# A strip loop's value unit issued straight behind the scores, and a unit's decays ahead of ScalarE's first copy

## The chip, the cores and the metric

The kernel runs on one core of a Trainium2 chip. The metric is the device time of the program, in microseconds (us). Five engines work side by side, each through its own instructions in order, and wait for each other on semaphores: TensorE (PE: matmuls, its weight loads in rows PEld), VectorE (DVE), ScalarE (ACT), GpSimd (POOL) and SyncE (SP, which issues DMAs). The kernel before took 2348.93 us, the median of 3 runs (2347.29 to 2349.18).

## The reference, cut to what matters

One layer over 32 batches of 64 tokens of width 256: cross-attention to 1601 context rows for each batch, a selective scan, and 64 experts with top-8 routing. The change lies in the attention:

```
q  = qdq(layernorm(x)) @ qdq(wq).T + bq          # 16 heads of 16
k, v = split(ctx @ wkv.T + bkv)                  # 1601 rows of 256 each
attn = softmax(q @ k.T / 4)
o    = attn @ v
x    = x + qdq(o) @ qdq(wp).T + bp
x    = x + scan(layernorm(x)) ; x = x + experts(layernorm(x))
# scan: h = exp(dt * A) * h + dt * x * B ; y = h . C
```

## The kernel before, in words

The tokens go in 16 pairs of batches (128 tokens). The attention of a pair is 16 strips: for each batch, each half of the heads (step), 4 strips of two heads each. A strip is 128 rows (two heads by 64 tokens) against 1604 key columns. One loop over G runs through the strips, one slot for each G; what the text calls slot s is G modulo 16. In a slot:

- TensorE: `scores(G)` (12 matmuls into the four-bank tensor S, line 618); `turn(G, 0..3)`: the probabilities of strip G-1 turned by 13 transposes in four groups of 4 or 3 (line 628); `v_mm`: a unit of values, two tiles of 128 context rows (line 601), in slots 1 to 7 for the pair's second batch and 9 to 15 for the next pair's first; `times_v(G)`: 12 to 16 products of turned probabilities and values into O (line 646); `k_mm(G + 4)`: the keys of a strip four ahead (line 591). Slots 0 and 8 have no value unit (`NO_VALUES`).
- ScalarE: `ot_up_` copies a finished O, `turned(G, k)` copies the four turned groups to SBUF (line 780), `soft(G)` takes the exponential of S (line 788), `k_up` writes the rounded keys (line 772), `decay` writes exp(dt A) of one scan unit (line 805, 4 instructions in each of slots 8 to 15).
- VectorE: `strip_max(G)` (line 958, 1604 columns of S), `v_up` copies a value unit to SBUF (line 952), `k_low` writes the keys' remainder (line 942), and between these the mixer work of the pair before: norms, routing (`rest_a`, `rest_b`) and the scan units (`scan_unit`).

S must be read by both `strip_max` and `soft` before the next scores may overwrite it. Everything else that TensorE writes, other than O, goes through a ring of three PSUM banks W0 to W2 (`BANKS = 3`). `jobs_at(G)` lists a slot's jobs in TensorE's order: T (a turned group), V (a value unit), K (keys) and small ones (O, oqT, proj, ln2T, xp, dt, XQ, Q, yT, ln3T, logits, pos, from the table `MIX` by slot and place). Job n takes bank n modulo 3, and `take` makes TensorE wait until job n-3 has been copied out: by ScalarE if that was a T, by VectorE otherwise (`freed_by`). So the order of jobs decides which copy each job waits for. In `jobs_at`, place 0 lies between the second and the third turned group, place 1 behind the fourth, place 2 behind the keys. Nothing plans at run time: the order is written out. Each engine's order has to agree with the list.

Of the kernel before, what the change touches and what calls it, by code (L numbers as in the profile page):

```python
# [60 lines left out]
UNITS = 2 * NS // QS  # L61
FIRST_DECAY = 4
# [16 lines left out]
def in_flight(G):  # L79

    return [(G - 1 - k, k) for k in range(STRIPS) if 0 <= G - 1 - k < ALL_STRIPS]


def values_at(G):

    i, slot = divmod(G, SLOTS)
    if 1 <= slot <= 7 and i < PAIRS:
        return i, 1, slot - 1
    if slot >= 9 and i + 1 < PAIRS:
        return i + 1, 0, slot - 9  # L90
    return None
# [20 lines left out]
def jobs_at(G):  # L112

    turns = [("T", G, k) for k in range(STRIPS)] if 0 < G <= ALL_STRIPS else []
    v = [("V",) + values_at(G)] if values_at(G) else []
    keys = [("K", G + STRIPS)] if G + STRIPS < ALL_STRIPS else []
    if G % SLOTS in NO_VALUES:
        return turns + small_at(G, 0) + keys + small_at(G, 1)
    return turns[:2] + small_at(G, 0) + v + turns[2:] + small_at(G, 1) + keys + small_at(G, 2)


def freed_by(job):
# [83 lines left out]
def mixer_phase(nc, io, dram):  # L206
    with ExitStack() as ctx:
# [338 lines left out]
        def _(pe):  # L546
# [181 lines left out]
            for G in range(END):  # L728
                if G < ALL_STRIPS:
                    scores(G)  # L730
                if 0 < G <= ALL_STRIPS:
                    turn(G, 0)
                    turn(G, 1)
                if G % SLOTS in NO_VALUES:
                    if 0 < G <= ALL_STRIPS:
                        turn(G, 2)
                        turn(G, 3)
                    if in_flight(G):
                        times_v(G)
                    small(G, 0)  # L740
                else:
                    small(G, 0)
                    if values_at(G):
                        v_mm(*values_at(G))
                    if 0 < G <= ALL_STRIPS:
                        turn(G, 2)
                        turn(G, 3)
                    small(G, 1)
                    if in_flight(G):
                        times_v(G)  # L750
                if G + STRIPS < ALL_STRIPS:
                    k_mm(G + STRIPS)
                small(G, 1 if G % SLOTS in NO_VALUES else 2)
# [3 lines left out]
        def _(act):  # L757
# [54 lines left out]
            for G in range(END):  # L812
                p, m = mixer_at(G)
                strip = 0 < G <= ALL_STRIPS
                if 0 <= G - STRIPS - 1 < ALL_STRIPS:
                    ot_up_(G - STRIPS - 1)
                if strip:
                    turned(G, 0)
                    turned(G, 1)
                if strip and G % SLOTS in NO_VALUES:  # L820
                    turned(G, 2)
                scanned = p is not None and 0 <= m - FIRST_DECAY < UNITS
                if scanned:
                    decay(p, m - FIRST_DECAY, 0)
                if G < ALL_STRIPS:
                    soft(G)
                if m == 3 and p is not None:
# [10 lines left out]
                    turned(G, 3)  # L838
                if G + STRIPS < ALL_STRIPS:
                    k_up(G + STRIPS)  # L840
                if scanned:
                    decay(p, m - FIRST_DECAY, 1)
                if m == 14 and p is not None:

                    act.wait_ge(dve_up, dve_at(p, "LOGITS"))
# [6 lines left out]
        def _(dve):  # L852
# [282 lines left out]
            for G in range(END):  # L1135
                i, slot = divmod(G, SLOTS)
                p, m = mixer_at(G)
                mix, nxt = p is not None, i + 1 < PAIRS
                v = values_at(G)
                if G < ALL_STRIPS:  # L1140
                    strip_max(G)
                if m == 0:
                    link = Chain(dve, dve_b, p, B_LINKS, pause[:]) if mix else None
                for job in small_at(G, 0):
                    if job[0] == "O":
                        norm_o(job[1])
                if slot == 8 and nxt:
                    x_up(i + 1)
                if mix and m < 15:
                    rest_a(p, m, link)  # L1150
                if v:
                    v_up(*v)
                if slot == 8 and i >= 2:
                    route_end(i - 2, route_link)
                if mix and m == 15:
# [423 lines left out]
```

## Time and profile before

| | |
|---|---|
| median of 3 runs | 2348.93 us |
| the profiled execution | 2351.5 us |
| its span (first to last instruction) | 2349.8 us |
| PE busy | 2113.0 us (90%) |
| DVE busy | 1754.1 us (75%) |
| ACT busy | 1439.1 us (61%) |
| mean granted TensorE clock | 0.968 of 2.4 GHz |
| exponentials, line 788 | 256, 1599 ns each |
| row maxima, line 958 | 256, 1820 ns each |
| value copies, line 952 | 224, 650 ns each |

The strip loop fills most of the span, the experts and the combination follow from about 1880 us on. The busy share of TensorE counts overlapping, pipelined matmuls; where it stands near the whole of a stretch, the engine has hardly any gap there. A timeline row gives the start of a group of like instructions, the time from its first start to its last end, the engine, the line and the operation, and in brackets the idle time of the engine just before with what ended it. On TensorE the next group starts before the last one's end, so intervals are best taken from start to start.

### The profile page before, as it was taken

How to read it: one execution, taken by the hardware profiler on the slowest of the kernel's cores; microseconds unless marked ns; L12 is line 12 of the kernel's file. 1: busy time of each engine (PE TensorE's matmuls, PEld its weight loads, DVE VectorE, ACT ScalarE, POOL GpSimd, SP SyncE). 2: the span in 40 equal slices, each digit the busy share in tenths (PEclk: the TensorE clock that was granted, in tenths of full speed). 3: DMA queues.
4: the chain of work that ended last, by engine and by line, in shares of the span. 5: the costliest groups of instructions: out<-in, count | busy, mean ns of one | idle time of the engine just before them, and what ended most of it. 6: DMA issues, size and time to landing. Idle time of an engine off the chain costs nothing. (4 is left out here: it accounts for less than half of the span.)

```text
span 2349.8 us, 56067 instructions
## 1 busy us (share of the span) xinstructions
PE 2113.0 (90%) x21448; PEld 1465.6 (62%) x21448; DVE 1754.1 (75%) x3728; ACT 1439.1 (61%) x3012; POOL 679.3 (29%) x710
## 2 busy tenths in 40 slices
PE   5999999999999999999999999999994099989966
PEld 3666666666666666666666666666663077767644
DVE  4557888879797978888887979797887555555536
ACT  1667776768676767677776768676775044434423
POOL 1002040303031221303040303131221447767760
PEclk9999999999999999999999999999997599999988
DMA  6465763323231313232232323131311165566638
GB/s 190 192 241 208 273 209 127 103 57 115 76 87 70 91 70 86 79 100 89 74 102 54 106 81 93 70 89 68 89 52 46 48 189 184 185 208 190 190 104 322
DMA packets 132712, 294.17 MB, mean 125 GB/s; under 512 B 21899, under 2 KB 89143, under 8 KB 126304
## 3 DMA queue, kind: packets, MB, share of 16 engines
q1 hardware_dynamic: 114016, 255.89, 34.8%
q0 software_dynamic: 18432, 34.69, 4.2%
q8 instruction: 174, 2.85, 0.5%
q14 instruction: 90, 0.74, 0.1%
HBM read 165.40 MB, written 108.27 MB: 116 GB/s over the span
## 5 line engine op out<-in xcount | busy, mean ns | idle before, releaser
L788 ACT ACTIVATE sb_probs<-S,sb_negmax 128x1604 f32<-128x1604 f32 x256 | 409.3, 1599 | 225.0 <-DVE sb_negmax L958 224.5
L780 ACT ACTIVATE sb_probsT<-W 128x384 f32<-128x384 f32 (+1 forms) x1024 | 473.5, 513 | 68.0 <-PE W L628 65.3
L628 PE MATMUL W<-sb_ident,sb_probs 128*128 128x128 f32 (+1 forms) x3328 | 478.6, 280 | 29.1 <-DVE sb_ln2T L980 15.5
L958 DVE TENSOR_REDUCE sb_negmax<-S 128x1 f32<-128x1604 f32 x256 | 465.9, 1820 | 1.3
L628 PEld LDWEIGHTS W<-sb_ident,sb_probs 128*128 128x128 f32 (+1 forms) x3328 | 363.7, 139 | 147.8 <-issue 68.5
L601 PE MATMUL W<-sb_wkv_in,sb_ctx 128*128 128x256 f32 (+1 forms) x1664 | 409.4, 388 | 4.8 <-ACT sb_probsT L780 2.6
L591 PE MATMUL W<-sb_ctx,sb_wkv_in 128*32 128x401 f32 x4096 | 398.0, 503 | 3.0 <-DVE sb_V L952 3.0
L601 PEld LDWEIGHTS W<-sb_wkv_in,sb_ctx 128*128 128x128 f32 (+1 forms) x1664 | 292.9, 186 | 67.2 <-ACT sb_probsT L780 19.1
L772 ACT ACTIVATE sb_K_hi<-W,sb_pair_cols 128x401 fp32r<-128x401 f32 x256 | 152.9, 597 | 238.8 <-PE W L591 238.8
L1292 POOL DMA_INDIRECT y_scratch<-sb_ys,sb_places x256 | 261.4, 1021 | 113.3 <-issue 62.9
L942 DVE SCALAR_TENSOR_TENSOR sb_K_lo<-W,sb_pair_cols,sb_K_hi 128x401 fp32r<-128x401 f32 x256 | 161.9, 632 | 153.6 <-ACT sb_K_hi L772 153.3
L500 POOL TENSOR_TENSOR sb_bx<-sb_u,sb_BC 128x512 f32<-128x512 f32 x128 | 164.8, 1304 | 363.8 <-DVE sb_u L1081 233.1
L646 PE MATMUL O<-sb_probsT,sb_V 128*32 128x128 f32 (+1 forms) x6656 | 243.9, 276 | 0.0
L591 PEld LDWEIGHTS W<-sb_ctx,sb_wkv_in 128*32 128x32 f32 x4096 | 131.5, 110 | 115.1 <-issue 102.9
L646 PEld LDWEIGHTS O<-sb_probsT,sb_V 128*32 128x32 f32 (+1 forms) x6656 | 173.2, 109 | 47.8 <-issue 34.8
L952 DVE COPY sb_V<-W 128x512 f32<-128x512 f32 (+1 forms) x224 | 145.7, 650 | 42.2 <-PE W L601 38.9
L512 POOL DMA_INDIRECT xe_scratch<-sb_row,sb_sc_idx x128 | 139.9, 1093 | 43.8 <-issue 31.0
L1364 ACT ACTIVATE sb_ys<-Y 128x512 f32<-128x512 f32 x64 | 38.3, 598 | 180.1 <-DMA y_scratch<-sb_ys,sb_places 170.3
L618 PEld LDWEIGHTS S<-sb_K_hi,sb_Q_hi 32*128 32x128 f32 x1024 | 49.6, 181 | 158.1 <-issue 155.6
L1332 PE MATMUL Y<-sb_wd,sb_hid 96*128 96x256 f32 x512 | 126.6, 391 | 16.5 <-DVE sb_ys L1406 16.4
L528 POOL TENSOR_TENSOR sb_st<-sb_st,sb_neg_half 128x1 f32<-128x1 f32 x16 | 8.8, 548 | 416.7 <-DVE sb_st L1062 416.7
L523 POOL TENSOR_TENSOR sb_st<-sb_st,sb_neg_half 128x1 f32<-128x1 f32 x16 | 9.1, 567 | 397.1 <-DVE sb_st L874 397.1
(187 smaller groups left out, 2951.4 us busy)
## 6 DMA issues: line engine op xcount, KB each, us to landing
sb_ctx<-ctxT SPq DMA_DIRECT2D x32, 1604.0 KB, 7.7
xe_scratch<-sb_none SPq DMA_DIRECT2D x32, 1088.0 KB, 12.6
sb_xg<-xe_scratch SPq DMA_DIRECT2D x64, 544.0 KB, 4.2
sb_BC<-bc_scratch SPq DMA_DIRECT2D x32, 1024.0 KB, 6.3
sb_Q_hi<-sb_q_hi SPq DMA_DIRECT2D x128, 128.0 KB, 4.2
sb_Q_lo<-sb_q_lo SPq DMA_DIRECT2D x128, 128.0 KB, 5.1
y_scratch<-sb_none SPq DMA_DIRECT2D x16, 1024.0 KB, 11.3
sb_rows<-y_scratch SPq DMA_DIRECT2D x16, 1024.0 KB, 8.5
```

What stands on the lines that cost most here:

```text
L500: pool.tensor_tensor(bx[:, mine, :], u[:, h, :].unsqueeze(1).to_broadcast([P, QS, P]), BC[:, mine, :], ALU.mult).then_inc(pool_up, 1)
L591: ins = pe.matmul(W[32 * c:32 * c + 32, 0:CK], wkv_in[:, k, w0:w0 + 32], ctx_t[b][:, k, c * CK:(c + 1) * CK], start=(k == 0), stop=(k == D ...
L601: ins = pe.matmul(W[0:keys_in(t), n * D:(n + 1) * D], ctx_t[b][:, k, t * P:t * P + keys_in(t)], wkv_in[:, k, D:2 * D], start=(k == 0), sto ...
L628: ins = pe.transpose(W[0:keys_in(t), at * P:(at + 1) * P], probs[n % 2][:, t * P:t * P + keys_in(t)], ident[:])
L646: ins = pe.matmul(O[32 * s:32 * s + 32, 0:P], V[b][0:keys_in(t), t, g * P + 32 * s:g * P + 32 * s + 32], probsT[k][n % (k + 1)][0:keys_in( ...
L772: act.activation(K_hi[:, s, 0:CK], ring[bank_of("K", n)][:, 0:CK], ACT.Identity, bias=pair_cols[:, g * STRIPS + s:g * STRIPS + s + 1]).the ...
L780: act.activation(probsT[k][n % (k + 1)][:, 0:wide], ring[bank_of("T", G, k)][:, 0:wide], ACT.Copy)\
L788: act.activation(probs[n % 2][:].rearrange("p (c k) -> p c k", c=QUADS), scores_of, ACT.Exp, bias=negmax[:, slot:slot + 1], accum_out=den[ ...
L942: dve.scalar_tensor_tensor(K_lo[:, s, 0:CK], bank("K", n)[:, 0:CK], pair_cols[:, g * STRIPS + s:g * STRIPS + s + 1], K_hi[:, s, 0:CK].bitc ...
L952: dve.tensor_copy(V[b][0:keys_in(tiles[-1]), tiles[0]:tiles[-1] + 1, :].rearrange("p t d -> p (t d)"), bank("V", pair, b, unit)[0:keys_in( ...
L958: dve.tensor_reduce(negmax[:, slot:slot + 1], scores_of, AX.XY, ALU.max, negate=True).then_inc(max_done, 1)
L1292: pool.indirect_dma_start(dram["y"], bass.IndirectOffsetOnAxis(ap=places[e % 4][:, c:c + 1], axis=0), ys[n][:, c, :], None, bounds_check=T ...
```

## The change

In every slot with a value unit, the unit's matmuls are issued right behind the scores, ahead of all four turned groups, where before they stood between the second and the third. VectorE copies the unit right behind the row maximum, ahead of the small copies and the mixer's work at that place. The list `jobs_at` is changed accordingly, and with it which job precedes which by three in the ring. Apart from this, ScalarE does all four decay instructions of a unit in one piece behind `ot_up_`, ahead of the first copy of turned probabilities; before, two stood ahead of the exponential and two behind `k_up`.

```diff
@@ jobs_at
-    return turns[:2] + small_at(G, 0) + v + turns[2:] + small_at(G, 1) + keys + small_at(G, 2)
+    return v + turns[:2] + small_at(G, 0) + turns[2:] + small_at(G, 1) + keys + small_at(G, 2)
@@ tensor
                 if G < ALL_STRIPS:
                     scores(G)
+                if values_at(G):
+                    v_mm(*values_at(G))
                 if 0 < G <= ALL_STRIPS:
                     turn(G, 0)
                     turn(G, 1)
...
                     small(G, 0)
-                    if values_at(G):
-                        v_mm(*values_at(G))
                     if 0 < G <= ALL_STRIPS:
                         turn(G, 2)
                         turn(G, 3)
@@ scalar
                     ot_up_(G - STRIPS - 1)
+                if p is not None and 0 <= m - FIRST_DECAY < UNITS:
+                    for part in range(2):
+                        decay(p, m - FIRST_DECAY, part)
                 if strip:
                     turned(G, 0)
                     turned(G, 1)
                 if strip and G % SLOTS in NO_VALUES:
                     turned(G, 2)
-                scanned = p is not None and 0 <= m - FIRST_DECAY < UNITS
-                if scanned:
-                    decay(p, m - FIRST_DECAY, 0)
...
                 if G + STRIPS < ALL_STRIPS:
                     k_up(G + STRIPS)
-                if scanned:
-                    decay(p, m - FIRST_DECAY, 1)
@@ vector
                     link = Chain(dve, dve_b, p, B_LINKS, pause[:]) if mix else None
+                if v:
+                    v_up(*v)
                 for job in small_at(G, 0):
...
                     rest_a(p, m, link)
-                if v:
-                    v_up(*v)
```

How instructions stand on TensorE in slot 15 of a pair, before. S are the scores, `W<-sb_ident,sb_probs` the turned groups, `W<-sb_wkv_in,sb_ctx` the value unit, `W<-sb_ctx,sb_wkv_in` the keys; `ring_free_act` and `ring_free_dve` say whose copy the bank is waited for:

```order
L618 MATMUL S<-sb_K_hi,sb_Q_lo 128x400 x3
L628 MATMUL W<-sb_ident,sb_probs 128x128 [waits exp_done,ring_free_act]
L628 MATMUL W<-sb_ident,sb_probs 128x128 x2
L628 MATMUL W<-sb_ident,sb_probs 128x128 [waits ring_free_act]
L628 MATMUL W<-sb_ident,sb_probs 128x128 x3
L601 MATMUL W<-sb_wkv_in,sb_ctx 128x256 [waits ctx_in0,ring_free_dve]
L601 MATMUL W<-sb_wkv_in,sb_ctx 128x256 x3
L628 MATMUL W<-sb_ident,sb_probs 128x128 [waits ring_free_act]
L628 MATMUL W<-sb_ident,sb_probs 128x128 x2
L628 MATMUL W<-sb_ident,sb_probs 128x128 [waits ring_free_act]
```

The same place now:

```order
L618 MATMUL S<-sb_K_hi,sb_Q_lo 128x400 x3
L601 MATMUL W<-sb_wkv_in,sb_ctx 128x256 [waits ctx_in0,ring_free_act]
L601 MATMUL W<-sb_wkv_in,sb_ctx 128x256 x3
L628 MATMUL W<-sb_ident,sb_probs 128x128 [waits exp_done,ring_free_act]
L628 MATMUL W<-sb_ident,sb_probs 128x128 x2
L628 MATMUL W<-sb_ident,sb_probs 128x128 [waits ring_free_dve]
L628 MATMUL W<-sb_ident,sb_probs 128x128 x3
L628 MATMUL W<-sb_ident,sb_probs 128x128 [waits ring_free_dve]
L628 MATMUL W<-sb_ident,sb_probs 128x128 x2
L628 MATMUL W<-sb_ident,sb_probs 128x128 [waits ring_free_act]
```

The value unit is ahead; the third turned group now takes the value unit's own bank and waits for VectorE's copy of it, where before it waited for ScalarE's copy of the first group, and the keys took the value unit's bank.

ScalarE in slot 15, before, from the exponential of one strip to the next (`sb_soft<-sb_dt_,sb_A` are the decays, `sb_OT<-O` is `ot_up_`):

```order
L772 ACTIVATE sb_K_hi<-W,sb_pair_cols 128x401 [waits s_done,ring_full]
L805 ACTIVATE sb_soft<-sb_dt_,sb_A 128x128 x2
L797 ACTIVATE sb_OT<-O 32x128 [waits pv_done]
L780 ACTIVATE sb_probsT<-W 128x384 [waits pv_done,ring_full]
L780 ACTIVATE sb_probsT<-W 128x512 [waits pv_done,ring_full]
L805 ACTIVATE sb_soft<-sb_dt_,sb_A 128x128 [waits dve_up]
L805 ACTIVATE sb_soft<-sb_dt_,sb_A 128x128
L788 ACTIVATE sb_probs,sb_den<-S,sb_negmax 128x1604 [waits ring_full,max_done]
```

And now:

```order
L772 ACTIVATE sb_K_hi<-W,sb_pair_cols 128x401 [waits s_done,ring_full]
L797 ACTIVATE sb_OT<-O 32x128 [waits pv_done]
L805 ACTIVATE sb_soft<-sb_dt_,sb_A 128x128 [waits dve_up]
L805 ACTIVATE sb_soft<-sb_dt_,sb_A 128x128 x3
L780 ACTIVATE sb_probsT<-W 128x384 [waits pv_done,ring_full]
L780 ACTIVATE sb_probsT<-W 128x512 [waits pv_done,ring_full]
L788 ACTIVATE sb_probs,sb_den<-S,sb_negmax 128x1604 [waits ring_full,max_done]
```

The decays of a unit stand in one piece ahead of the first two copies, and nothing stands between those and the exponential.

VectorE in slot 7, before (`sb_z<-W` reads the small job dt, `sb_u` is the end of the chain that the decays need):

```order
L958 TENSOR_REDUCE sb_negmax<-S 128x1 [waits s_done]
L1020 TENSOR_SCALAR sb_z<-W,sb_cols 128x128 [waits ring_full]
L1021 TENSOR_SCALAR sb_z<-W,sb_cols 128x128 [waits dve_b]
L1024 SCALAR_TENSOR_TENSOR sb_soft<-sb_z 128x256 [waits ring_free_dve]
L952 COPY sb_V<-W 128x512 [waits pv_done,ring_full]
L1075 TENSOR_SCALAR sb_soft<-sb_soft 128x256 [waits act_up]
```

And now (the same functions, two lines earlier in the file):

```order
L956 TENSOR_REDUCE sb_negmax<-S 128x1 [waits s_done]
L950 COPY sb_V<-W 128x512 [waits pv_done,ring_full]
L1018 TENSOR_SCALAR sb_z<-W,sb_cols 128x128 [waits ring_full]
L1019 TENSOR_SCALAR sb_z<-W,sb_cols 128x128 [waits dve_b]
L1022 SCALAR_TENSOR_TENSOR sb_soft<-sb_z 128x256 [waits ring_free_dve]
L1073 TENSOR_SCALAR sb_soft<-sb_soft 128x256 [waits act_up]
```

The copy of the value unit stands ahead of the three instructions that read dt.

## Rows read from the trace of the kernel before

**Rows 1.** The page, busy time of each engine (share of the span), instructions.
```profile
PE 2113.0 (90%) x21448; PEld 1465.6 (62%) x21448; DVE 1754.1 (75%) x3728; ACT 1439.1 (61%) x3012; POOL 679.3 (29%) x710
```

**Rows 2.** Windows: one pair; stretch, its length, busy us, granted clock, DMA share, GB/s.
```profile
1025.23:1134.92 109.69, 106.10 (x1228) 71.98 (x1224) 92.53 (x195) 78.03 (x164) 24.82 (x23) 1.00 0.29 85
```

**Rows 3.** Timeline, TensorE: first scores of pair 1 and of pair 15.
```profile
150.85 0.46 PE L618 MATMUL S<-sb_K_hi,sb_Q_hi 32*128 32x402 f32 x4
...
1683.36 0.45 PE L618 MATMUL S<-sb_K_hi,sb_Q_hi 32*128 32x402 f32 x4
```

**Rows 4.** Waits of TensorE in that pair: us in total, times, longest.
```profile
PE W L628 <- DVE sb_ln2T L980: 1.1, 1, 1.1
```

**Rows 5.** Timeline, TensorE, a slot 15 and the start of the next slot.
```profile
1019.00 0.46 PE L618 MATMUL S<-sb_K_hi,sb_Q_hi 32*128 32x402 f32 x4
...
1019.76 0.98 PE L628 MATMUL W<-sb_ident,sb_probs 128*128 128x128 f32 x7
1020.58 1.92 PE L601 MATMUL W<-sb_wkv_in,sb_ctx 128*128 128x256 f32 x8
1022.33 0.82 PE L628 MATMUL W<-sb_ident,sb_probs 128*128 128x128 f32 x6
...
1025.23 0.45 PE L618 MATMUL S<-sb_K_hi,sb_Q_hi 32*128 32x402 f32 x4
```

**Rows 6.** Timeline, VectorE, the same slot 15.
```profile
1019.82 0.63 DVE L942 SCALAR_TENSOR_TENSOR sb_K_lo<-W,sb_pair_cols,sb_K_hi 128x401 fp32r<-128x401 f32 x1
1020.36 1.82 DVE L958 TENSOR_REDUCE sb_negmax<-S 128x1 f32<-128x1604 f32 x1
1022.53 0.69 DVE L952 COPY sb_V<-W 128x512 f32<-128x512 f32 x1 [0.35 <-PE W L601]
```

**Rows 7.** Timeline, ScalarE, the same slot 15.
```profile
1020.63 0.98 ACT L780 ACTIVATE sb_probsT<-W 128x384 f32<-128x384 f32 x2
1021.50 0.69 ACT L805 ACTIVATE sb_soft<-sb_dt_,sb_A 128x128 f32<-128x128 f32 x2
1022.22 1.60 ACT L788 ACTIVATE sb_probs<-S,sb_negmax 128x1604 f32<-128x1604 f32 x1
```

**Rows 8.** Timeline, TensorE, slot 1 (from 1030.50) and slot 3 (from 1045.69).
```profile
1030.50 0.46 PE L618 MATMUL S<-sb_K_hi,sb_Q_hi 32*128 32x402 f32 x4
...
1034.36 0.93 PE L628 MATMUL W<-sb_ident,sb_probs 128*128 128x128 f32 x7
...
1045.69 0.45 PE L618 MATMUL S<-sb_K_hi,sb_Q_hi 32*128 32x402 f32 x4
...
1048.98 0.82 PE L628 MATMUL W<-sb_ident,sb_probs 128*128 128x128 f32 x6
...
1050.78 1.55 PE L591 MATMUL W<-sb_ctx,sb_wkv_in 128*32 128x401 f32 x16 [0.18 <-DVE sb_V L952]
```

**Rows 9.** Timeline, VectorE, slots 1 and 3.
```profile
1032.22 1.82 DVE L958 TENSOR_REDUCE sb_negmax<-S 128x1 f32<-128x1604 f32 x1
...
1048.29 1.83 DVE L958 TENSOR_REDUCE sb_negmax<-S 128x1 f32<-128x1604 f32 x1
1050.04 0.68 DVE L952 COPY sb_V<-W 128x512 f32<-128x512 f32 x1
```

**Rows 10.** Timeline, TensorE, slot 10, the small job O.
```profile
987.97 0.33 PE L656 MATMUL W<-sb_ident,sb_OT 128*128 128x128 f32 x1 [0.80 <-DVE sb_K_lo L942]
```

**Rows 11.** Timeline, ScalarE, slot 8 (its scores start at 972.53).
```profile
973.98 1.36 ACT L780 ACTIVATE sb_probsT<-W 128x512 f32<-128x512 f32 x3 [0.41 <-PE W L628]
975.21 0.70 ACT L805 ACTIVATE sb_abar<-sb_dt_,sb_A 128x128 f32<-128x128 f32 x2
```

**Rows 12.** Timeline, TensorE, 13 transposes at clock 1.0, and at 0.5.
```profile
1776.96 1.96 PE L628 MATMUL W<-sb_ident,sb_probs 128*128 128x128 f32 x13
...
1781.77 3.06 PE L628 MATMUL W<-sb_ident,sb_probs 128*128 128x128 f32 x13 [2.06 <-ACT sb_probs L788]
```

**Rows 13.** Windows: the experts and the combination, columns as in rows 2.
```profile
1900.00:2350.00 450.00, 386.71 (x1852) 292.04 (x1849) 248.16 (x571) 178.48 (x370) 275.88 (x321) 0.94 0.61 198
```

## The prediction, made before the changed kernel ran

> **What bounds the kernel now.** First the page's busy times: TensorE has 90% of the span, VectorE 75%, ScalarE 61% [rows 1]. Then the windows, pair by pair: of a pair's 109.69 us TensorE is busy for 106.10 at a granted clock of 1.00, VectorE for 92.53 [rows 2]. Its gaps make 3.6 us of the pair; the longest are 1.1 us in slot 6 [rows 4] and 0.8 us in slot 10, for VectorE's keys [rows 10]. So in the strip loop TensorE is the bound and has nearly no gap. The loop is regular: pair 1 starts at 150.85 and pair 15 at 1683.36, 14 pairs in 1532.5 us [rows 3], 109.5 each. Last the timelines of single slots, from start to start on TensorE. Below, all times inside a slot count from the start of its scores.
>
> In slot 15 [rows 5] TensorE issues scores at 0, two turned groups at 0.76, the value unit at 1.58, the other two groups at 3.33, and the next scores at 6.23. VectorE [rows 6] starts the row maximum at 1.36. It does not wait for the scores there: it comes from the keys' remainder of the slot before (0.82 to 1.45), which comes from ScalarE's key copy, which comes from the end of TensorE's keys. The maximum takes 1.82, then VectorE stands 0.35 for the value unit and copies it from 3.53 to 4.22. Nobody waits for that copy but the keys, which come behind the products.
>
> **The change, part by part.** The work is the same: no matmul, copy or DMA is added or removed, and no DMA queue is touched. Only the order moves, and with it the banks.
>
> *The value unit first.* Issuing V ahead of two groups costs TensorE nothing by itself; the sum of the three is the same, 3.33 us to the third group in slot 15. What changes is who waits for the copy. With three banks and V, T0, T1, T2 in line, T2 gets V's bank. It waits for VectorE's copy, which stands behind the row maximum. Where a small job stands behind T1, that job gets V's bank and waits instead, with T2 behind it in line. The earliest issue of that job after the scores is
>
> start of the maximum + 1.75 (the next VectorE instruction starts that long after it: 1048.29 to 1050.04, rows 9) + 0.68 (the copy) + 0.06 (the copy's end at 1050.72 to the keys that waited for it at 1050.78, rows 8 and 9) = start of the maximum + 2.49.
>
> In slot 15 that is 1.36 + 2.49 = 3.85 against 3.33 [rows 5, 6]: 0.5 us of stall. Behind the waiting T2 stand T3, the products, the keys and the next scores; the keys' end then sets the next key copy, remainder and maximum. Nothing in this chain can catch up: it is the loop's new cycle, 1.36 + 2.49 + 2.9 (third group to next scores) = 6.75 us. The 0.35 us that VectorE stood for V goes, but it stands ahead of a later wait now, for the keys.
>
> The same reading in each of the 14 slots with a value unit (of each the start of the maximum and of the third group; the first and the last, slots 1 and 15, have their rows, and slot 3). Where VectorE's backlog of scan work delays its maximum today (slots 10 to 12, 14 and 0, up to 0.9 us), the longer slots clear it, and I take the maximum at 1.34 to 1.43 there.
>
> - Slots 9, 11, 12, 13, 15: +0.64, +0.23, +0.28, +0.49, +0.50 = +2.14.
> - Slots 10 and 14, with the small job O: slot 10 today waits for the keys' remainder until 987.97 [rows 10]; that wait goes with the backlog: -0.24. Slot 14 has a short unit, +0.07. Together -0.17.
> - Slot 1: maximum at 1.72 [rows 9], small job at 4.24, third group at 4.51 against 3.86 [rows 8]: +0.65. In the same way slots 2, 4, 5, 6, 7: +0.50, +0.27, +0.42, +0.69, +0.59. Together +3.12. In slot 6 the fourth group already waits for VectorE today, so only the difference counts.
> - Slot 3: VectorE starts the maximum at 2.60, since it normalises the next queries ahead of it [rows 9]. Third group at 5.09 against 3.29 [rows 8]: 1.80; today the keys wait for the same copy [rows 8], which takes back 0.35: +1.44.
>
> *The decays ahead of the first copy.* In slots 9 to 15 this is hidden. ScalarE has done the key copy and `ot_up_` at about 1.05, four decays take 1.3 (0.69 for two, rows 7), so it is free at 2.35. T0 now comes behind V, so its copy can start at about 3.1, as against 1.63 [rows 7]. The exponential moves: today it starts at 3.22 [rows 7], now behind T1's copy at about 3.95. It ends at about 5.65, and the next scores come at 6.7 or later, so a full 1 us of cover is left. T3's copy ends at about 6.5, the next key copy wants ScalarE at 6.9: 0.4 us of cover, the thinnest. If it is gone, each 0.1 us late there is 0.1 us on every slot.
>
> In slot 8 there is no V to hide it. T3 needs the bank of T0, and T0's copy starts at 1.45 today [rows 11]. Now four decays stand ahead of it, and they wait for the end of the softplus chain of slot 7, which on VectorE moves back too (dt waits for the value copy, 1.41 + 2.49 = 3.9 as against 1.6). The chain also waits for ScalarE's exponential, which ends about as late as dt's readers, so I get the chain's end at 1.0, decays to 2.3, T0's copy to 2.9, T3 at 2.95 against 2.1: +0.85. Bounds: not below 0.85, since `ot_up_` ends at 1.05 anyway; up to 2.3 if the chain moves by as much as dt does beyond the slot's own growth (2.3 - 0.6 = 1.7), which would be 23 us in all.
>
> In slot 0 two decays of slot 15 no longer stand ahead of the first copies: -0.26.
>
> **Sum.** 2.14 - 0.17 + 3.12 + 1.44 + 0.85 - 0.26 = 7.12 us for each pair. For the 14 pairs from 1 to 14: 100. Pair 0 has no mixer work but the same norms of queries, and slots 2, 3 and 6 where these delay the maximum; the same reading gives 8. Pair 15 has no value units from slot 9 on: 6. Together 114 us. The profiled execution took 2351.5 us (its span 2349.8), so 2465.5 there, a factor 1.0485; on the median of 2348.93 that is 2463 us. The copies, groups and handoffs are measured; the starts of the maximum are what can be wrong. 0.1 us on them is 14 x 16 x 0.1 = 22 us in all. From both sides: if the maximum starts as today everywhere with no backlog cleared, some 1.5 us per pair more, +24; if the wait is shorter by 0.15 in each slot, -33.
>
> **The rivals.**
>
> *TensorE's clock falls* (8%). Today the loop runs at 1.00, which is 2.4 GHz, with waits of at most about 1 us. The same 13 transposes took 1.96 us at that clock and 3.06 behind a wait of 2.06 us, in a stretch granted 0.5, which is 1.2 GHz [rows 12]. In the stretch of experts, with TensorE busy 86% of the time, the mean is 0.94, so 12% of it is at the lower level [rows 13]. After the change the loop would be busy for 106.1 of 116.8 us, 91%, in gaps of half a microsecond to 1.8. If 12% of 1740 us fell to the lower level, each at 1.56 times the duration, 75 us come on top: 2538 us. Against it: waits of 0.8 and 1.1 us occur in each pair today [rows 4, 10] and the clock stays at 1.00 [rows 2].
> The Trainium skill, "TensorE: Matmul & The Clock Gate", section "A second HAM failure mode: psum-queue depth-cycling", describes this: a kernel that cycles through PSUM banks and idles briefly between its groups of matmuls was seen to swing between the clock's two levels. By that rule 2538 would be the forecast; the trace's loop, which cycles through three banks and idles briefly, does not agree so far, at 1.00 throughout.
>
> *ScalarE becomes late as well* (10%). The cover of 0.4 us ahead of the next key copy is gone, say by 0.3 us, in the 13 ordinary slots. That delays the maximum and with it the copy: 13 x 0.3 x 16 = 62 us on top, 2525.
>
> *VectorE gets ahead, and it is faster* (5%). If the value copy no longer waits for V, VectorE saves 0.35 in each scan slot; if that let the maximum start right at the scores' end, at 0.87 or earlier, the copy would be done when T2 wants its bank (0.87 + 2.49 = 3.36), and the wait in slot 10 and a few others would go, about 1 us a pair, 15 us: 2334. The point that decides is the start of the maximum: below 0.87 it is faster, above it a stall. Against it: the maximum stands behind the keys' remainder, which ends at 1.45 at the earliest and does not come sooner by this change.
>
> *It does nothing* (5%): the turned groups find their banks free because the copy comes earlier than I read, 2349.
>
> **How the numbers follow.** The forecast has 72%, the others 8, 10, 5 and 5. Within 0.2% is about what a measurement of this kernel can tell from no change. Slower by more than that: 72 + 8 + 10 = 90%; within: 5%; faster: 5%. Range: 2465 less 33 and some room for slots 3 and 8 gives 2425; upwards 24 and most of the way to the late ScalarE, 2515, which also takes in slot 8's upper bound. That holds the forecast and half of that rival.
>
> **What would show it.** In the profile after: TensorE's waits get a large new entry, transposes (line 628, and the small jobs) for VectorE's value copy (line 950), some 200 times and 100 to 150 us in total; a slot 15 of about 6.75 us; slot 3 of about 8.3; a pair of about 116.8; VectorE's wait for the value unit gone; the exponential starting at about 3.95 behind the copy of T1, not behind the maximum. ScalarE's wait for the keys stays above zero in ordinary slots. The clock at 1.00 in the loop. The prediction is wrong if the maximum starts well before 1.3, or if the third group is not held by the copy, or if ScalarE has no idle time left before line 772.

## The result and the profile after

The changed kernel took 2466.2 us (median of 4 runs, 2460.53 to 2472.05) against 2349.05 (4 runs, 2347.29 to 2349.94): a ratio of 1.0501, 95% interval 1.0486 to 1.0516. It is 117 us slower; the prediction said 2463 and 114. The profiled execution has a span of 2470.3 us. In experiment 1 below, one of four runs took 2932 us at a mean granted clock of 0.674; the other three took 2455.87 to 2459.42 us at 0.967 to 0.969, and its ratio is from these.

One pair in the windows view of the changed kernel (columns as in rows 2):

```profile
1095.45:1212.09 116.64, 105.36 (x1224) 72.36 (x1220) 92.42 (x195) 78.16 (x164) 24.08 (x23) 1.00 0.27 79
```

Against [rows 2] TensorE's and VectorE's work is the same and the pair is 6.95 us longer. The waits of TensorE in that pair:

```profile
PE W L628 <- DVE sb_V L950: 3.4, 6, 1.6
PE W L656 <- DVE sb_V L950: 3.3, 4, 1.1
PE W L663 <- DVE sb_V L950: 3.2, 3, 2.0
PE W L628 <- ACT sb_probsT L780: 0.8, 1, 0.8
PE W L691 <- DVE sb_V L950: 0.4, 1, 0.4
```

Fourteen waits, one for each slot with a value unit, are for VectorE's value copy: 10.3 us in a pair where [rows 2] has 3.6 us of gaps of all kinds. Over the whole loop there are 214 such waits, 155 us in all; the prediction said some 200 and 100 to 150 us. In a pair they are more than the 6.95 us of growth, since they take the place of most of those gaps. The one wait for ScalarE is slot 8's.

The timeline of TensorE in a slot 15 (answers to [rows 5]):

```profile
1088.60 0.46 PE L618 MATMUL S<-sb_K_hi,sb_Q_hi 32*128 32x402 f32 x4
...
1089.35 2.00 PE L601 MATMUL W<-sb_wkv_in,sb_ctx 128*128 128x256 f32 x8
1091.18 0.93 PE L628 MATMUL W<-sb_ident,sb_probs 128*128 128x128 f32 x7
1092.50 0.87 PE L628 MATMUL W<-sb_ident,sb_probs 128*128 128x128 f32 x6 [0.39 <-DVE sb_V L950]
...
1095.45 0.46 PE L618 MATMUL S<-sb_K_hi,sb_Q_hi 32*128 32x402 f32 x4
```

and VectorE there (answers to [rows 6]):

```profile
1090.03 1.82 DVE L956 TENSOR_REDUCE sb_negmax<-S 128x1 f32<-128x1604 f32 x1
1091.76 0.68 DVE L950 COPY sb_V<-W 128x512 f32<-128x512 f32 x1
```

The copy ends at 1092.44, the third group starts at 1092.50. The 0.35 us for which VectorE stood before the value unit are gone. The slot takes 6.85 us, as against 6.23. ScalarE there (answers to [rows 7]):

```profile
1089.65 1.28 ACT L805 ACTIVATE sb_soft<-sb_dt_,sb_A 128x128 f32<-128x128 f32 x4
1091.71 1.03 ACT L780 ACTIVATE sb_probsT<-W 128x384 f32<-128x384 f32 x2 [0.78 <-PE W L628]
1092.64 1.59 ACT L788 ACTIVATE sb_probs<-S,sb_negmax 128x1604 f32<-128x1604 f32 x1
...
1095.59 0.60 ACT L772 ACTIVATE sb_K_hi<-W,sb_pair_cols 128x401 fp32r<-128x401 f32 x1 [0.51 <-PE W L591]
```

The decays are hidden here (0.78 us idle behind them), the exponential starts at 4.04 us of the slot, and 0.51 us of cover are left ahead of the keys. Slot 3, where the maximum is late, has the row that answers to [rows 8]:

```profile
1121.75 0.88 PE L628 MATMUL W<-sb_ident,sb_probs 128*128 128x128 f32 x6 [1.58 <-DVE sb_V L950]
```

The slots one by one, from start to start of the scores, medians over pairs 2 to 14 (before; growth as the prediction had it; growth as measured):

| slot | 0 | 1 | 2 | 3 | 4 | 5 | 6 | 7 |
|---|---|---|---|---|---|---|---|---|
| before, us | 5.27 | 6.89 | 8.30 | 6.84 | 7.04 | 7.91 | 8.03 | 6.72 |
| predicted | -0.26 | +0.65 | +0.50 | +1.44 | +0.27 | +0.42 | +0.69 | +0.59 |
| measured | -0.26 | +0.58 | +0.44 | +1.36 | +0.26 | +0.13 | +0.69 | +0.60 |

| slot | 8 | 9 | 10 | 11 | 12 | 13 | 14 | 15 |
|---|---|---|---|---|---|---|---|---|
| before, us | 6.52 | 6.48 | 7.36 | 6.49 | 6.67 | 6.34 | 6.61 | 6.22 |
| predicted | +0.85 | +0.64 | -0.24 | +0.23 | +0.28 | +0.49 | +0.07 | +0.50 |
| measured | +1.08 | +0.24 | -0.13 | +0.37 | +0.30 | +0.53 | +0.08 | +0.63 |

Sum: 7.12 predicted, 6.90 measured. Pair 0 grew by 8.8, pair 1 by 9.1 and pair 15, to its slot 14, by 3.2 us. Five stretches at the lower clock, told below, cost some 1.6 us each; one lies in pair 1 and is in its 9.1, the other four make the rest. The loop grew by 117.5 us.

### The profile page after: what moved, and what is told of

Its sections match the earlier page's. It is cut to its first block and busy times, and to the rows that moved or that the text cites. A ratio compares the mean times of both kernels' runs of the same rounds, so it can differ in the third digit from the quotient of the medians.

```text
span 2470.3 us, 56068 instructions
## 1 busy us (share of the span) xinstructions
PE 2110.6 (85%) x21448; PEld 1475.2 (60%) x21448; DVE 1751.3 (71%) x3728; ACT 1439.8 (58%) x3012; POOL 678.3 (27%) x710
## 5 line engine op out<-in xcount | busy, mean ns | idle before, releaser
L780 ACT ACTIVATE sb_probsT<-W 128x384 f32<-128x384 f32 (+1 forms) x1024 | 479.1, 519 | 337.5 <-PE W L628 336.6
L628 PE MATMUL W<-sb_ident,sb_probs 128*128 128x128 f32 (+1 forms) x3328 | 463.9, 276 | 75.7 <-DVE sb_V L950 54.4
L628 PEld LDWEIGHTS W<-sb_ident,sb_probs 128*128 128x128 f32 (+1 forms) x3328 | 370.6, 139 | 148.8 <-DVE sb_V L950 78.0
L601 PE MATMUL W<-sb_wkv_in,sb_ctx 128*128 128x256 f32 (+1 forms) x1664 | 416.9, 392 | 0.0
L646 PE MATMUL O<-sb_probsT,sb_V 128*32 128x128 f32 (+1 forms) x6656 | 249.8, 279 | 0.0
```

The source lines that it names most:

```text
L601: ins = pe.matmul(W[0:keys_in(t), n * D:(n + 1) * D], ctx_t[b][:, k, t * P:t * P + keys_in(t)], wkv_in[:, k, D:2 * D], start=(k == 0), sto ...
L628: ins = pe.transpose(W[0:keys_in(t), at * P:(at + 1) * P], probs[n % 2][:, t * P:t * P + keys_in(t)], ident[:])
L646: ins = pe.matmul(O[32 * s:32 * s + 32, 0:P], V[b][0:keys_in(t), t, g * P + 32 * s:g * P + 32 * s + 32], probsT[k][n % (k + 1)][0:keys_in( ...
L780: act.activation(probsT[k][n % (k + 1)][:, 0:wide], ring[bank_of("T", G, k)][:, 0:wide], ACT.Copy)\
```

## The experiments

Each is compared with the kernel before on the same chip (2348 us there).

**1. The value unit first, the decays in their old place.**

```diff
@@ the changed kernel, scalar
-                if p is not None and 0 <= m - FIRST_DECAY < UNITS:
-                    for part in range(2):
-                        decay(p, m - FIRST_DECAY, part)
...
+                scanned = p is not None and 0 <= m - FIRST_DECAY < UNITS
+                if scanned:
+                    decay(p, m - FIRST_DECAY, 0)
                 if G < ALL_STRIPS:
                     soft(G)
...
                     k_up(G + STRIPS)
+                if scanned:
+                    decay(p, m - FIRST_DECAY, 1)
```

> The value unit first, as in the changed kernel, but the decays where they were before. Theory (the stall is the third ring job's wait for VectorE's value copy): the placement alone costs nearly all of the 117 us, 2465 us (2450 to 2480). Slot 8 goes back to about 6.5 us, which gives back some 13 us, but in slots 9 to 15 two decays stand ahead of the exponential behind T1's late copy, so ScalarE is late for the next keys by 0.1 to 0.2 us, which takes it away again. Rival (the decays ahead of the first copy are what costs): back to within 20 us of the kernel before, below 2370 us.

Measured: 2459.08 us, ratio 1.0451 (1.0374 to 1.0528). The placement of the value unit alone costs some 110 of the 117 us. The rival falls. Slot 8 went back to 6.71 us, but slot 9 took 7.41 instead of the changed kernel's 6.72, so the two together gained 0.2 us, no more. About 3 of the 7 us between this run and the changed kernel are the clock: three stretches at the lower level here, five there. The total came out as forecast, but not by the way forecast: ScalarE did lose its idle time ahead of the keys in slots 11, 12, 13 and 15, yet these slots took 6.92, 6.97, 6.87 and 6.85 us, at most 0.06 more than in the changed kernel. What took slot 8's gain away was slot 9's late maximum (1.88 us into the slot, as against 1.18), see 5.

**2. The decays' part alone,** in the kernel before.

```diff
@@ the kernel before, scalar
                     ot_up_(G - STRIPS - 1)
+                if p is not None and 0 <= m - FIRST_DECAY < UNITS:
+                    for part in range(2):
+                        decay(p, m - FIRST_DECAY, part)
...
-                    decay(p, m - FIRST_DECAY, 0)
...
-                    decay(p, m - FIRST_DECAY, 1)
```

> The decays' part of the change alone: all four ahead of the first copy in slots 8 to 15, the value unit in its old place. Theory: slot 8 pays 0.85 to 1.1 us as in the changed kernel, slot 9 gives 0.2 back, slot 0 gives 0.26 back: some 10 us, 2359 us (2352 to 2366). Rival (the two parts need each other, and the decays cost little without the value unit first): within 5 us of 2349.

Measured: 2363.97 us, ratio 1.0067 (1.0050 to 1.0084), 16 us. The direction holds and the time is within the range, 5 us above its middle. Slot 8 grew by 0.93 and slot 9 shrank by 0.29, as expected; slots 10 and 14 grew by 0.37 and 0.21, which I had not seen; slot 11 shrank by 0.15; and slot 0 kept its 5.27 us.

**3. As 2, with slot 8 in its old order.**

```diff
-                if p is not None and 0 <= m - FIRST_DECAY < UNITS:
+                scanned = p is not None and 0 <= m - FIRST_DECAY < UNITS
+                if scanned and G % SLOTS not in NO_VALUES:
                     for part in range(2):
                         decay(p, m - FIRST_DECAY, part)
...
+                if scanned and G % SLOTS in NO_VALUES:
+                    decay(p, m - FIRST_DECAY, 0)
...
+                if scanned and G % SLOTS in NO_VALUES:
+                    decay(p, m - FIRST_DECAY, 1)
```

> The value unit in its old place behind T1; all four decays ahead of ScalarE's first copy in slots 9 to 15, old order in slot 8. Theory: T0 and T1 are copied late (2.35 instead of 1.63 us) but before T2 and T3 want their banks (3.33 and 3.8), and slot 0 loses the two decays in front of its first copies (5.27 to 5.01 us): 15 x 0.26 = 4 us less, 2345 us. Rival (moving decays ahead of copies always delays the copies' waiters): 10 us or more slower.

Measured: 2355.87 us, ratio 1.0025 (1.0004 to 1.0047). A miss: 8 us slower, not 4 faster. TensorE's waits in a pair show why:

```profile
PE W L628 <- DVE sb_ln2T L983: 1.1, 1, 1.1
PE W L601 <- ACT sb_probsT L780: 0.9, 1, 0.9
PE W L656 <- DVE sb_K_lo L945: 0.8, 1, 0.8
PE S L618 <- ACT sb_probs L788: 0.3, 1, 0.3
```

The second is new in this size (0.2 us in the kernel before): in slot 14 the value unit waits for ScalarE's copy of a turned group. With a small job behind T1, the old order gives the value unit T1's bank, and T1's copy now stands behind four decays. In the changed kernel the value unit is first and does not meet this. And slot 0 did not gain: with the decays out of ScalarE's way, the next scores wait for the exponential (the last of these rows), which stands behind a maximum that starts at 1.59. In the changed kernel VectorE's backlog is cleared and the maximum starts at 1.33. Run 1 has that earlier maximum with the decays in their old place, and its slot 0 takes 5.13 us. So the -0.26 in the changed kernel needs both parts: the decays alone give nothing, the maximum alone 0.14.

**4. As 3, with slots 10 and 14 in the old order too.**

```diff
-                if scanned and G % SLOTS not in NO_VALUES:
+                if scanned and G % SLOTS not in (8, 10, 14):
...
-                if scanned and G % SLOTS in NO_VALUES:
+                if scanned and G % SLOTS in (8, 10, 14):
```

> The value unit in its old place, the four decays ahead of ScalarE's first copy in slots 9, 11, 12, 13 and 15 only. In the run with slots 10 and 14 among them, these two grew by 0.37 and 0.20 us; reading: with a small job behind T1 the value unit takes T1's bank, and T1's copy had moved from 2.0 to 2.7 us. Theory: slots 10 and 14 go back to 7.36 and 6.61 us and the time to 2347 us (2343 to 2350). Rival (slot 10 grew because of slot 9's decays, not its own): slot 10 stays at 7.7 us, 2354.

Measured: 2351.58 us, ratio 1.0009 (1.0000 to 1.0018). Slots 10 and 14 took 7.36 and 6.61 us: the reading of T1's bank holds. The total came out above the range since slot 15 took 6.59 us, 0.37 more than before: it now has slot 14's last two decays and its own four ahead of its first copy. Slot 11 grew by 0.10 in the same place behind slot 10, and slot 12 gave that back. Slot 0 took 5.02 us here, with its maximum at 1.33 and no decays ahead of its copies, which bears out the reading in 3.

**5. The changed kernel with slot 8's decays in the old order** (the edit of 3, in the changed kernel).

> The changed kernel, with the decays of slot 8 (no value unit there) where they were before: two ahead of the exponential, two behind the keys. Theory: slot 8 of the changed kernel is 7.60 us against 6.52, because T0's copy stands behind four decays and T3 waits for T0's bank; slot 9 gained 0.4 us from it since VectorE had caught up. So about 0.8 us less a pair, 12 us: 2454 us, slot 8 at 6.5 to 6.7. Rival (slot 8 is long because VectorE's chain of slot 7 moved back): slot 8 stays above 7.2 us and the time within 5 us of 2466.

Measured: 2460.89 us, ratio 1.0464 (1.0404 to 1.0524). Slot 8 went to 6.71 us, so its 7.60 was T0's copy behind the decays. But slot 9 went from 6.72 to 7.41 and took 0.7 of the 0.9 us back. VectorE's long work in slot 8 (routing and the next queries) is followed by slot 9's maximum, which starts at 1.2 us of a slot 9 when slot 8 is long and at 1.9 when it is short. So the decays' net cost in the changed kernel is about 0.2 us a pair, 3 us in all. The forecast had counted all of slot 8's 0.8 us, and so the run came out 7 us above it. This run has four stretches at the lower clock instead of five.

**6. The value unit second,** between T0 and T1, ScalarE as in 5.

```diff
-    return v + turns[:2] + small_at(G, 0) + turns[2:] + ...
+    return turns[:1] + v + turns[1:2] + small_at(G, 0) + turns[2:] + ...
@@ tensor
+                if 0 < G <= ALL_STRIPS:
+                    turn(G, 0)
                 if values_at(G):
                     v_mm(*values_at(G))
                 if 0 < G <= ALL_STRIPS:
-                    turn(G, 0)
                     turn(G, 1)
```

> As the run before this one, with the value unit between the first and the second turned group: one ring job more now stands between it and the one that takes its bank (T3 or, with a small job ahead, T2). Theory: that job is due at about 3.8 us and the copy is done at 3.85, so ordinary slots lose about 0.1 us and only slots 2, 3, 6 and 9 much (0.3, 1.0, 0.4 and 0.2 us): 2375 us (2360 to 2390). Rival (any value unit ahead of its old place costs in proportion to how far it is moved): half of the loss stays, 2405 us.

Measured: 2404.21 us, ratio 1.0220 (1.0160 to 1.0280). The forecast of the total is missed, and by the total the rival is hit to the microsecond. The slots do not fit the rival, by which every slot would keep about half of its loss: slot 3 kept 1.03 of 1.36 us and slot 2 only 0.06 of 0.44, and slot 5 got shorter by 0.17. They fit the formula, but not my use of it. Slots 2, 3 and 6 grew by 0.06, 1.03 and 0.39 us. Slots 13 and 15 grew by 0.20 and 0.21 and not by 0.1: in slot 15 T3 starts at 3.66 us in the kernel before, so it is due well ahead of the 3.8 that I had estimated from the value unit's place; here it starts at 3.81, 0.05 us behind the copy's end, and the products behind it 0.21 us later than before. Slots 1 and 4, which I had left out, grew by 0.36 and 0.22: with a small job behind T1 it is T2 that takes the value unit's bank. In slot 1 the formula gives 1.72 + 2.49 = 4.21 for it, as against 3.86 before, and it starts at 4.19. Slots 8 and 9 grew by 0.39 and 0.60, where the theory had 0.2 for slot 9 only; no run tells their causes apart. Two stretches of pairs 1 to 14 are at the lower clock, some 3 us of the 56.

**7 and 8. One VectorE instruction more ahead of each value copy,** once in the changed kernel, once in the kernel before.

```diff
@@ v_up
                 tiles = V_UNITS[unit]
+                if pair > 0 or b == 1:
+                    after(dve, idled, lags[0])
+                    dve.memset(idle_w[:], 0.0).then_inc(idled, 1)
+                    lags[0] += 1
                 dve.wait_ge(ring_full, full_at("V", pair, b, unit))
```

> The changed kernel with one more VectorE instruction, a memset of 128x256 (I expect some 0.3 us, the trace will tell) right ahead of each value copy in the loop. Theory: the copy ends that much later and every slot with a value unit grows by it one for one: 217 x 0.3 = 65 us, 2531 us. Rival (VectorE has slack in its waits for the keys, so that a little more work there is hidden): below 2480.

> The same added memset in the kernel before, where it stands ahead of VectorE's wait for the value unit. Theory: in ordinary slots it falls into that wait of 0.35 us and into the 0.5 us that the keys leave; only slots 3 (keys already wait for the copy) and those where VectorE is behind (2, 6, 10) feel it, 3 x 0.3 x 15 = 14 us at most, 2349 to 2363 us. Rival (VectorE's busy time counts wherever it is added): 65 us, 2414.

Measured: 2515.65 us in the changed kernel (1.0719, 1.0700 to 1.0738), 49 us on top of its 2466; 2370.67 us in the kernel before (1.0100, 1.0083 to 1.0117), 23 us on top. In the timeline of VectorE:

```profile
1009.53 1.82 DVE L962 TENSOR_REDUCE sb_negmax<-S 128x1 f32<-128x1604 f32 x1
1011.35 0.27 DVE L950 MEMSET sb_idle_w<- 128x256 f32 x1
1011.54 0.63 DVE L956 COPY sb_V<-W 128x512 f32<-128x512 f32 x1
```

The copy now ends 2.64 us behind the maximum's start (1009.53 to 1012.17), as against 2.41 in the changed kernel (1090.03 to 1092.44). 13 of its 14 value slots grew by 0.21 to 0.23 us, slots 0, 8 and 10 not at all: one for one, as the theory has it. In slot 10 the maximum now starts 0.22 us earlier (1.37, not 1.59), since the longer slots ahead of it clear more of VectorE's backlog. The forecast took 0.3 us for each of 217 copies and came out too high; 202 x 0.22 is 44, and the loop has eight stretches at the lower clock where the changed kernel has five, some 5 us more. In the kernel before only slots 1, 2, 3, 6, 11 and 15 grew by 0.2 to 0.34 and slot 5 by 0.1, the other seven by nothing. That is above the theory's range (its upper end was 14 us) and far below the rival's 65. Slots 1, 5, 11 and 15 were not in my list and slot 10 should not have been. In slots 11 and 15 the maximum started later (1.97 and 1.64 us, as against 1.63 and 1.36), so VectorE had no slack there; I read that as backlog of the scan units, and no run tests it.

**9. The rounding of the next queries at the end of slot 7 instead of slot 5,** in the kernel before.

```diff
-                if slot == 5 and nxt:
+                if slot == 7 and nxt:
                     round_q(q_link)
```

> The kernel before with the rounding of the next queries on VectorE moved from the end of slot 5 to the end of slot 7. Theory (it is the start of the row maximum that sets who waits): slot 6's maximum starts at 1.3 instead of 2.3 us, its fourth group no longer waits for the small copy, slot 6 goes from 8.03 to 7.05 us as it is in the last pair, which rounds nothing: 14 x 0.98 = 14 us less, 2335 us. In slot 8 the later maximum is covered by VectorE's 0.9 us wait for the turned queries. Rival (the lateness moves with the work to slot 8 and 9): within 4 us of 2349.

Measured: 2386.52 us, ratio 1.0168 (1.0150 to 1.0186). Slot 6 went from 8.03 to 7.05 us, as forecast to the hundredth. But slot 8 went from 6.52 to 9.87, and the forecast is missed. VectorE in that slot 8:

```profile
985.09 0.93 DVE L866 TENSOR_SCALAR sb_x_q<-sb_x_q,sb_st 128x256 f32<-128x256 f32 x1
986.05 1.25 DVE L867 TENSOR_SCALAR sb_x_q<-sb_x_q 128x256 f32<-128x256 f32 x1
987.35 1.23 DVE L868 TENSOR_SCALAR sb_x_q<-sb_x_q,sb_st 128x256 f32<-128x256 f32 x1
```

and GpSimd beside it:

```profile
984.60 5.10 POOL L500 TENSOR_TENSOR sb_bx<-sb_u,sb_BC 128x512 f32<-128x512 f32 x4 [14.65 <-DVE sb_u L1081]
```

The same three instructions take 0.34, 0.29 and 0.35 us in the kernel before, where GpSimd is idle:

```profile
959.11 0.34 DVE L866 TENSOR_SCALAR sb_x_q<-sb_x_q,sb_st 128x256 f32<-128x256 f32 x1
959.49 0.29 DVE L867 TENSOR_SCALAR sb_x_q<-sb_x_q 128x256 f32<-128x256 f32 x1
959.82 0.35 DVE L868 TENSOR_SCALAR sb_x_q<-sb_x_q,sb_st 128x256 f32<-128x256 f32 x1
```

Beside GpSimd's four products each of the three ends 0.14 to 0.15 us behind the end of one of these (987.16 and 987.30 for the second). They take 2.4 us more than alone, and with the 1.0 us that they take alone this is slot 8's growth of 3.4 us. The kernel before meets the same thing in small in its own slot 8, where a product runs from 977.08 to 978.34:

```profile
977.17 1.20 DVE L1114 TENSOR_SCALAR sb_topf<-sb_topf 128x8 f32<-128x8 f32 x1
```

In run 9, where GpSimd is done by then, that instruction takes 0.17 us. The rest of the loss is the clock: behind slot 8's two waits of 1.31 and 1.85 us TensorE was granted 0.50 for a stretch in ten of the 14 pairs, from pair 5 on, which makes them 112.7 instead of 111.2 us, 15 us in all. Without it the run would still be more than 20 us slower than the kernel before. The place was wrong, not the theory of the maximum.

**10. All work on the next queries put into waits that VectorE has,** in the kernel before.

```diff
+                if slot == 5 and nxt:
+                    round_q(q_link)
                 if mix:
                     rest_b(p, m, link)
...
+                if slot == 1 and nxt:
+                    q_link = moments_q(i + 1)
+                if slot == 2 and nxt:
+                    norm_q(i + 1, q_link)
                 if G + STRIPS < ALL_STRIPS:
                     k_low(G + STRIPS)
...
-                if slot == 1 and nxt:
-                    q_link = moments_q(i + 1)
-                if slot == 2 and nxt:
-                    norm_q(i + 1, q_link)
-                if slot == 5 and nxt:
-                    round_q(q_link)
```

> The kernel before, with VectorE's three pieces of work on the next queries moved from behind the keys' remainder into waits that VectorE has anyway: the moments of slot 1 and the normalisation of slot 2 ahead of the keys' remainder (it waits there for ScalarE's keys), the rounding of slot 5 ahead of the mixer's step that waits for the projection. Theory (the start of the row maximum decides who waits): the maxima of slots 2, 3 and 6 start at 1.3 instead of 2.06, 2.60 and 2.30 us, and the slots take what they take in the last pair, which has no queries to prepare: 7.77, 6.36 and 7.05 us instead of 8.30, 6.84 and 8.03. 2.0 us a pair, 14 pairs: 28 us less, 2321 us (2315 to 2330). Rival (the work is not free anywhere, VectorE only gets late elsewhere): within 5 us of 2349 or slower.

Measured: 2321.78 us, ratio 0.9881 (0.9865 to 0.9896): 27 us faster than the kernel before, and the fastest kernel here. Slots 2, 3 and 6 take 7.77, 6.42 and 7.05 us, as forecast but for 0.06 in slot 3; no other slot changed by more than 0.02. A stretch of one pair's length, by the windows:

```profile
1000.00:1107.75 107.75, 105.68 (x1222) 72.15 (x1220) 92.71 (x196) 78.18 (x165) 24.82 (x23) 1.00 0.28 85
```

**11. The same move in the changed kernel.**

> The same move of the work on the queries, in the changed kernel. Theory (third job behind the value unit = start of the maximum + 2.49 us): the stalls of slots 2, 3 and 6 shrink one for one with the maximum's start, by 0.7, 1.25 and 0.95 us: 2.9 us a pair, 41 us in all, 2425 us (2415 to 2435), more than the same move gives in the kernel before. Rival (the stall has a part that does not hang on the maximum, such as ScalarE's later copies): the gain is the same 28 us as there, 2438.

Measured: 2414.06 us, ratio 1.0278 (1.0264 to 1.0292), 52 us below the changed kernel, twice what the move gives in the kernel before. Slots 2, 3 and 6 shrank by 0.75, 1.22 and 0.98 us, one for one with the maximum's start (to 1.32, 1.39 and 1.32). That makes 41 of the 52. The rest is the clock, below, with 8 us, and pair 0 with 3.

## Why the prediction was right

**The third ring job's wait.** This is nearly the whole of it: the 14 slots with a value unit make 6.08 of the 6.90 us of a pair. There are 14 waits a pair for line 950, the copy's end and the group's start 0.06 us apart as in [rows 8, 9]. Run 1 shows that it needs no decays, runs 7 and 11 that it follows the copy's end one for one, from either side: a copy that is later by 0.23 us lengthens a slot by 0.22, an earlier maximum by 1.2 us shortens slot 3 by 1.2.

**The formula, start of the maximum + 2.49.** It gave the third group at 3.85 in slot 15, it starts at 3.90 there. The clearing of VectorE's backlog, which I had only argued, is there in slots 12, 14 and 0 (maximum at 1.33, 1.32 and 1.33, before 1.59, 1.54 and 1.58). In slot 10 it is not complete (from 2.29 to 1.59 and not to 1.43 or less), so that slot shrank by 0.13 and not by 0.24. In slots 11 and 15 the maximum starts at 1.44 and 1.43, since VectorE waits 0.41 us in the slot before for the small job O, which TensorE issues only after the value copy. That is a term I had not counted. These two slots grew by 0.14 and 0.13 us more than forecast; in slot 15 the later maximum is 0.07 of it, and the runs do not tell the rest apart.

**Slot 5** was sized wrong, +0.13 and not +0.42. Today the projection takes the value unit's bank there and already waits for its copy. The waits in a pair of the kernel before have it, and I passed over it since it is put down to the weight loads:

```profile
PEld W L674 <- DVE sb_V L952: 0.3, 1, 0.3
```

It is the discount that I gave slot 3 and not slot 5. (In slot 3 I called 0.35 us the keys' wait where [rows 8] have 0.18; it is rather that the interval from the third group to the keys is 1.80 us there and 1.43 in slot 15. The slot grew by 1.36, as against 1.44.)

**Slots 8 and 9,** 1.49 predicted, 1.32 measured, but split otherwise (1.08 and 0.24). The mechanism in slot 8 was right: T3 waits 0.84 us for T0's copy, behind the decays. ScalarE there, and TensorE:

```profile
1040.88 1.28 ACT L805 ACTIVATE sb_abar<-sb_dt_,sb_A 128x128 f32<-128x128 f32 x4 [0.18 <-DVE sb_u L1079]
1042.19 1.36 ACT L780 ACTIVATE sb_probsT<-W 128x512 f32<-128x512 f32 x3
```

```profile
1042.84 0.55 PE L628 MATMUL W<-sb_ident,sb_probs 128*128 128x128 f32 x3 [0.84 <-ACT sb_probsT L780]
```

The decays wait 0.18 us for the softplus chain, which I had put at the same time as `ot_up_`. What I missed is that VectorE's work in slot 8 is fixed, so a longer slot 8 brings slot 9's maximum forward. Runs 1 and 5 show this from the other side: the decays cost 0.9 us in slot 8 (7.60 and 6.71 us) and only about 0.2 us in the sum.

**Slot 0.** The number was right by luck, for the reason was only half of it. By the decays alone, as the prediction had it, the slot gains nothing (runs 2 and 3); VectorE's earlier maximum alone gives 0.14 (run 1), and both together the 0.26.

**ScalarE's cover** was 0.5 us instead of 0.4 in slot 15 and at least 0.4 in each of slots 8 to 15. Slot 7 is the exception: there ScalarE goes from the last turned group (to 1039.78) to the keys (1039.81) without a pause, where the kernel before had 0.45 us. By my own sign that was a warning, but the key copy starts 0.14 us behind the next scores' start there and 0.15 in the kernel before, so nothing came of it. The rival of a late ScalarE did not happen.

**The clock** rival came true in small. In the changed kernel's loop five stretches from pair 1 on have a granted clock of 0.50, the lower level of 1.2 GHz, where the loop of the kernel before has none. Each begins in a slot 6, behind that slot's wait of 2.02 us, the longest in a pair. The timeline, and the windows:

```profile
909.86 0.44 PE L663 MATMUL W<-sb_ident,sb_ln 128*128 128x128 f32 x2 [2.02 <-DVE sb_V L950]
```

```profile
911.00:914.40 3.40, 3.40 (x40) 2.82 (x43) 1.24 (x8) 1.06 (x4) 0.00 (x0) 0.50 0.00 0
```

Such a pair takes 118.2 us instead of 116.6. Five times 1.6 is 8 us of the 117. Only 5 of 14 such waits of slot 6 had it; in run 11, where slot 6's wait is 1 us shorter, no stretch of the loop is at the lower level. Without them the change would cost 109 us, 5 under the forecast of 114; with them it is 3 over. So that the total came within 3 us is in part luck: an effect that the sum left out made up for slots sized too large. "TensorE: Matmul & The Clock Gate" of the Trainium skill says in "A second HAM failure mode: psum-queue depth-cycling" that brief idling between groups of matmuls in a ring of banks made the clock swing. By that rule, waits of 0.3 to 1.6 us in each value slot would do it; the trace does not agree for these, and agrees only for the wait of 2 us, and there in 5 cases of 14.

**The range and the rest.** Pair 0 (8 predicted, 8.8), pair 15 (6 and 3.2) and pair 1 (7 and 9.1, of which 1.5 are its stretch at the lower clock) even out. The whole lies well inside the range of 2425 to 2515.

## What to carry to other kernels

In a ring of n buffers that several kinds of job share, each job waits for the copy of the job n places ahead, so moving one job past others changes whom its neighbours wait for as well: here, in an ordinary slot, all six jobs (V, T0 to T3, K) wait for another one than before. The mover's own late copy lands on the job n places behind it. Before such a move, take the time at which the moved job's copy ends (here: the long instruction ahead of it on the copying engine plus the copy) and the time at which the job n places behind is due; the difference is the price for each turn, if it is positive. Take both times from the trace and not from the order alone: in run 6 I estimated a due time too late by 0.15 us and left two slots out, and the forecast was missed. And the place to gain was elsewhere: work that stands between one engine's last input and the instruction that the others wait for goes into a wait that this engine has anyway, which gave 1.2% without touching the order of the ring.

## What the runs showed of the hardware that was not expected

VectorE's fp32 tensor_scalar on SBUF of 128x256 took 0.93, 1.25 and 1.23 us beside GpSimd's tensor_tensor of 1.3 us, and 0.29 to 0.35 us without (run 9). VectorE's tensor_reduce and a copy from PSUM kept their time beside the same GpSimd instructions (1.82 and 0.42 us in the kernel before, at 973.86 and 976.60, with products from 973.37 to 978.34). A tensor_scalar of only 128x8 did not: 1.20 us beside a product, 0.17 without. The Trainium skill, "SBUF — State Buffer", section "SBUF: two separate sides", in its list "Reading the diagram", says that VectorE in a two-port mode and GpSimd share a pair of ports as an exclusive lock, held for the whole instruction. The trace agrees in that each of the three took about as long as one of GpSimd's products and ended 0.15 us behind one; that they run in such a mode no run here shows.

TensorE's granted clock fell to 0.50 for single stretches of some 3 us in the midst of a dense loop, each at a cost of 1.5 to 1.7 us. In pairs 1 to 14 it did so behind the 2.02 us wait of slot 6 in 5, 3 and 4 of 14 cases (the changed kernel, runs 1 and 5), behind one of 1.79 us in 2 of 14 (run 6), behind waits of 1.36, 1.80 and 2.24 us in 2, 3 and 3 of 14 (run 7), and behind 1.31 and 1.85 us in one slot in 10 of 14 (run 9). It never did behind slot 3's 1.58 us in the changed kernel, nor in run 11, whose longest wait is 1.04 us. So the length of the wait alone does not tell, and what else decides stays open.
